# A clip handed from VectorE to GpSimd in the tile loop of a gated mixture of experts

## The reference, cut to what matters

```python
def swiglu(h):
    g = jnp.minimum(h[..., ::2], LIMIT)
    l = jnp.clip(h[..., 1::2], -LIMIT, LIMIT)        # the clip of the linear part, LIMIT = 7
    return g * jax.nn.sigmoid(ALPHA * g) * (l + 1.0)
...
h1 = jnp.einsum('td,efd->etf', xt, w1) + b1[:, None, :]
h3 = jnp.einsum('td,efd->etf', xt, w3) + b3[:, None, :]
a = swiglu(h1 * h3)
y = jnp.einsum('etf,edf->etd', a, w2) + b2[:, None, :]
routed = jnp.einsum('te,etd->td', cw, y)              # cw: two experts of eight for each token
```

## Time and profile before

| what | value |
|---|---|
| timed runs, median (lowest to highest) | 2465.71 us (2459.22 to 2470.34) |
| profiled execution, first to last instruction | 2596.9 us |
| mean granted TensorE clock in it | 0.812 of full speed |
| PE, DVE, ACT, POOL busy in it | 2013.5, 1771.5, 1399.1, 1150.4 us |
| second phase of the first gated mixture, first to last clip | 172.16 to 305.41 us |
| second phase of the second, first to last clip | 1186.53 to 1318.5 us |
| POOL busy from 171.25 to 315.74 us | 76.11 us in 78 transfers |
| POOL busy from 1185.62 to 1328.08 us | 76.42 us in 78 transfers |

### The profile page before, as it was taken

The page is one execution under the profiler, slowest core; times in us unless marked ns, Lnnn a source line. Parts: engine busy times, 40 slices in busy tenths (PEclk is TensorE's granted clock), DMA queues, the critical chain, the costliest instruction groups (busy, mean ns, idle before and its releaser), DMA issues. The chain is left out here.

```text
span 2596.9 us, 85429 instructions
## 1 busy us (share of the span) xinstructions
PE 2013.5 (78%) x34490; PEld 1682.7 (65%) x34490; DVE 1771.5 (68%) x4346; ACT 1399.1 (54%) x2304; POOL 1150.4 (44%) x1073
## 2 busy tenths in 40 slices
PE   3767569999999998577738899564666689768895
PEld 2557468888888887456726799452222278647895
DVE  4666578888888888666755444676999965454443
ACT  1546534444455554345725455257999956545452
POOL 3645545666656665463535466355000000045463
PEclk8778889999999999578868999786555556669997
DMA  5122310000000000012241222202333220021324
GB/s 123 39 77 72 92 58 1 0 0 0 0 0 0 0 0 2 22 58 76 73 149 49 73 76 63 76 1 35 63 53 61 49 65 8 3 91 42 86 78 122
DMA packets 112885, 125.53 MB, mean 48 GB/s; under 512 B 24248, under 2 KB 94504, under 8 KB 112064
## 3 DMA queue, kind: packets, MB, share of 16 engines
q1 hardware_dynamic: 91760, 84.85, 13.5%
q0 software_dynamic: 18176, 37.79, 4.4%
q10 hardware_dynamic: 2768, 0.55, 0.2%
HBM read 60.00 MB, written 46.20 MB: 41 GB/s over the span
## 5 line engine op out<-in xcount | busy, mean ns | idle before, releaser
L2623 DVE CUSTOM_DVE_ANT_0 be_logs<-be_joint,be_logs 128x1024 f32<-128x1024 f32 x256 | 293.3, 1220 | 10.2 <-ACT be_logs L2606 9.1
L2606 ACT ACTIVATE be_logs<-be_joint,b_tiny 128x1024 f32<-128x1024 f32 x256 | 283.8, 1114 | 19.6 <-PE be_joint L2591 11.8
L2591 PE MATMUL be_joint<-be_parts_k,be_parts_q 64*128 64x512 f32 x512 | 202.3, 789 | 108.8 <-DVE be_sums L2623 91.4
L451 POOL DMA_INDIRECT d_pairs<-s_y_tile,s_x_tiles x156 | 178.0, 1141 | 128.1 <-DVE s_y_tile L1426 101.8
L2591 PEld LDWEIGHTS be_joint<-be_parts_k,be_parts_q 64*128 64x128 f32 x512 | 73.7, 285 | 237.3 <-DVE be_sums L2623 216.5
L451 POOL DMA_INDIRECT d_pairs<-g_y_tile,g_x_tiles x156 | 152.5, 978 | 166.6 <-ACT g_y_tile L901 122.5
L1260 PE MATMUL s_ps_y<-s_down,s_a_tile 128*128 x1248 | 151.8, 275 | 0.0
L1426 DVE TENSOR_SCALAR s_y_tile<-s_ps_y,s_x_tiles 128x128 f32<-128x128 f32 x156 | 47.6, 347 | 147.8 <-PE s_ps_y L1260 100.8
L1260 PEld LDWEIGHTS s_ps_y<-s_down,s_a_tile 128*128 128x128 f32 x1248 | 145.9, 192 | 0.0
L1540 PE MATMUL m_front<-m_xnT,m_w_rot 128*128 128x128 f32 x1024 | 143.4, 284 | 3.2 <-DVE m_turned_q L1857 3.2
L1336 ACT ACTIVATE s_a_tile<-s_ps_h,s_tile_bias 128x256 f32<-128x256 f32 x312 | 122.3, 475 | 32.8 <-PE s_ps_h L1243 32.6
(11 more groups left out here) (504 smaller groups left out, 6271.2 us busy)
## 6 DMA issues: line engine op xcount, KB each, us to landing
g_x_tiles<-d_rows SPq DMA_DIRECT2D x78, 132.0 KB
s_x_tiles<-d_rows SPq DMA_DIRECT2D x78, 132.0 KB
bw_v<-b_v SPq DMA_DIRECT2D x64, 68.0 KB, 2.1
d_rows<-d_rows SPq DMA_DIRECT2D x32, 132.0 KB
s_down<-L_ffn_We SPq DMA_DIRECT2D x16, 256.0 KB, 5.4
be_parts_q<-be_high_q SPq DMA_DIRECT2D x64, 64.0 KB, 2.3
be_parts_q<-b_soft_q SPq DMA_DIRECT2D x64, 64.0 KB, 2.3
be_parts_k<-be_high_k SPq DMA_DIRECT2D x60, 64.0 KB, 2.3
```

The lines of the kernel that those rows point to most:

```text
L451: nc.gpsimd.indirect_dma_start(out=pairs[:, :], out_offset=bass.IndirectOffsetOnAxis(ap=x_tile[i % LOADS_AHEAD][:, h, D:D + 1].bitcast(U32 ...
L2591: last = nc.tensor.matmul(joint_ps[k % DEPTH][:, a, :], parts[b % 2][0][rows, i * P:(i + 1) * P], parts[b % 2][1][rows, half * 512:(half + ...
L2606: nc.scalar.activation(logs[k % DEPTH][:, :, :], joint_ps[k % DEPTH][:, :, :], ACT.Ln, bias=A.tiny[:, :]).then_inc(s.log_ready, 1)
L2623: nc.vector.tensor_tensor_reduce(out=flat, in0=joint_ps[k % DEPTH][:, :, :].rearrange("p a j -> p (a j)"), in1=flat, scale=1.0, scalar=0.0 ...
```

## The change

The clip at line 1055 leaves DVE's queue and comes into POOL's, as a new function `tile_linear` with the same two operations on the same 128x256 elements. POOL's order in the second phase becomes: clip of tiles 0, 1, 2; from then on, for i from 3 to 38, the two transfers of tile i-3 and the clip of tile i; at the end the transfers of tiles 36, 37, 38. The clip waits for the linear product of its tile, and for `a_tile` of two tiles earlier, which read the same buffer. On DVE the second half of the product gains a wait for the clip of two tiles earlier, which reads the buffer that this half writes.

```diff
-            for i in range(MAX_TILES):
+            def tile_linear(i):
+                b = i % 2
+                pool.wait_ge(s.tile_prod_l, i + 1)
+                wait(pool, s.tile_a, i - 1)
+                nc.gpsimd.tensor_scalar(linear_tile[b][:, :], prod_tile[b][:, 1, :], 7.0, -7.0, ALU.min, ALU.max).then_inc(s.tile_linear, 1)
+
+            for i in range(MAX_TILES):
+                if i > 2:
+                    dispatch.pool_tile_back(pool, i - 3, K.pairs, x_tile, y_tile)
+                tile_linear(i)
+            for i in range(MAX_TILES - 3, MAX_TILES):
                 dispatch.pool_tile_back(pool, i, K.pairs, x_tile, y_tile)
...
                 for part in range(2):
                     dve.wait_ge(s.tile_third, 2 * i + part + 1)
-                    if part == 0:
-                        wait(dve, s.tile_sig, i - 1)
+                    wait(dve, s.tile_linear if part else s.tile_sig, i - 1)
...
-                dve.wait_ge(s.tile_prod_l, i + 1)
-                nc.vector.tensor_scalar(linear_tile[b][:, :], prod_tile[b][:, 1, :], 7.0, -7.0, ALU.min, ALU.max).then_inc(s.tile_linear, 1)
```

## The result

The changed kernel takes 2500.22 us (median of 4 runs, 2494.51 to 2506.61) against 2468.03 for the kernel before (median of 4 runs): ratio 1.0131, 95% interval [1.0099, 1.0162], so 24 to 40 us slower. The forecast was 2533, in a range from 2455 to 2590. Slower was right, and so was the mechanism, POOL's pace; of the 67 us that the forecast added, 32 came.

What follows compares the result with a forecast made beforehand. The prediction took POOL's transfers, 2.52 us a tile, to pace the timed runs, and added 72 clips at 0.04 + 0.89 = 0.93 us, 67 us, to 2465.71 for 2533 us, in a range from 2455 to 2590.

Steps and rivals of the forecast that it cites:

- The holes: Gated tile phases: DVE's waits, such as 3.50 us, about every 10 us when recorded; timed runs taken to have none.
- a ceiling on the rate of work while it is recorded: Reason given for the gated phase's holes, which lift its mean from 2.5 to 3.5 us a tile.
- the span forecast: Recorded span of the changed kernel: to stay about 2590 to 2620 us while the median rises to 2533.
- DVE's relief is worth nothing: DVE's turn falls from 2.45 to about 2.24 us without gain, since POOL's 2.52 us stand above both.
- 36 clips a call count: Clips 3 to 38 stand between POOL's transfer pairs, 72 in all at 0.93 us: 67 us; clips 0 to 2 free.
- the price of the clip: POOL's 128x256 clip: 0.89 us, read half way between TENSOR_SCALAR rows of 0.559 us (128x128) and 1.564 us (128x512).
- The pauses: Around POOL's clip: 0.04 us ahead of it, 0.30 us behind it, with 0.76 us kept for the range.
- That DVE and POOL hold each other up: Tile phase: a clip waiting once for a DVE instruction of 0.42 us, up to 30 us more, inside the range.
- the cheap clip: Rival: POOL's clip costs 0.26 us like the cast, adding 22 us, 2487 us; chance 0.12.
- Holes of the kernel's own: Rival: timed runs have the gated phase's holes too, leaving POOL room for the clips; 7.6 us gained, 2458 us; chance 0.25.
- the dear clip: Rival: POOL's clip costs 1.564 us with a 0.76 us pause behind it, adding 148 us, 2614 us; chance 0.13.

Runs made afterwards that it cites:

- e2: Changed kernel with the linear part's clip left out on both engines, the product used unclipped: 2469.53 us, ratio 1.0010 to the kernel before.
- e1: The kernel before, unchanged, timed and recorded again for a second profile: 2467.36 us, ratio 1.0009.
- e5: Changed kernel with POOL multiplying by 0.5 in place of clipping, same size and place: 2544.98 us, ratio 1.0302 to the kernel before.
- e4: The changed kernel, unchanged, timed again beside the kernel before: 2506.38 us, ratio 1.0154 to the kernel before.

## Why the prediction came out as it did

- *The holes*: that the timed runs have none was right, and POOL's phase is 98.7 us without them (98.3 said); with e2, POOL and not DVE set the pace. The reason given, a ceiling on the rate of work while it is recorded, was wrong: e1 was recorded and has none. So this step came right partly by luck, and the span forecast from it, 2590 to 2620 us, missed (2504.8). What made the holes in the first recording stays open.
- *DVE's relief is worth nothing*: right (e2). DVE waits 1.04 us a turn for the clip; about 1 us was said, but by luck, from a pace of 3.45 us and a DVE turn of 2.24, where 3.12 and about 2.08 came.
- *36 clips a call count*: right. Those ahead of the first transfer cost at most about 1 us, the first pair starting at 160.75, after a wait for ACT, against 159.72 in e1.
- *The failed step is the price of the clip*: "I take 0.89, because the two neighbours are the same operation." They were the same opcode and other operations: a multiplication and a comparison of integers. The clip is a minimum and a maximum and takes 0.395 us. For a multiplication of that size 0.89 is near (0.867 in e5), though one of the two rows is none. This is a term of the sum mis-sized, 72 x (0.89 - 0.395) = 36 us too much; with 0.395 the prediction's own sum is 2465.71 + 72 x (0.04 + 0.395) = 2497.
- *The pauses*: 0.07 ahead of the clip for 0.04, 0.27 behind it for 0.30. Right to 0.01 in sum.
- *That DVE and POOL hold each other up* was kept for the range, at most 30 us, and left out of the sum. The form named there, a clip that waits for a DVE instruction, doesn't show: all clips last 394 to 405 ns. What is there is a longer transfer, 0.12 us a turn under the multiplication, 9 us; another 0.035 us, 2.5 us, for the transfer behind a computation had no term. The Trainium skill (SBUF — State Buffer, section Who interferes with whom) was cited for it; the trace agrees for the CAST (1.17 us when it began 0.05 us earlier) and for work with one operand from PSUM, which that section lets pass (0.96, or 0.995 behind a computation). For `tensor_tensor` with both inputs in SBUF it infers, though, that it doesn't hold up the making of a DMA's descriptors; here another operation with two such inputs, the multiplication (`scalar_tensor_tensor`), goes with 442 transfers of 1.10 or 1.22 us on the mean, so that inference doesn't carry over to it, and the measurement decides.
- *The sum again*, from measured terms: 72 x (0.07 + 0.395 + 0.27 - 0.30 + 0.155) = 42.5 us, to 2466.4 + 42.5 = 2509; measured 2506 and 2500.
- *The rivals*: the cheap clip (0.26 us, 2487) was nearer in price than the forecast, and stood on the cast's row and on the Trainium skill (GPSIMD Engine Reference, section Engine selection): one-input work "roughly line-rate". For minimum and maximum, 0.83 ns an element beside the cast's 1.01, the runs agree; for the multiplication, (1.564 - 0.867) / 256 = 2.7 ns (2.4 if the 0.07 us of the column in the longer row is taken off), they don't. That a row of the same name spoke against the rule was taken for more than it was; the smaller of the two, 0.559 / 128 = 4.4 ns an element where "near 3 to 4" was read, is a comparison. Holes of the kernel's own, and the dear clip, are out by e1 and e4.

## What to carry to other kernels

Before you price an operation by a row, read in the code which arithmetic that row does: a profile's opcode does not tell a minimum from a multiplication, and on one engine these differed by a factor of two. Where an engine sets the pace with a chain of short transfers, an instruction put between them costs its own time and more: 0.38 us for one of a single column, which itself takes 0.18. The short pauses between the transfers are no room for it; the clip came on top of them. So move work to an engine that idles in that stage, and not by its share of the span. Record a profile again before you explain stalls that no program line accounts for.

## What the runs showed of the hardware

- GpSimd's TENSOR_SCALAR, f32, 128 partitions: minimum and maximum take 0.184 us for 1 column, 0.395 for 256, 0.608 for 512; with one bound from a column in SBUF 0.469 for 256; a multiplication 0.867 for 256 and 1.564 for 512.
- An indirect transfer of this phase lasts 0.96 us on GpSimd, 0.995 right behind a computation on GpSimd, and up to 1.28 when DVE at its start works on operands that are all in SBUF. In the changed kernel the two meet in nearly every turn, since both follow GpSimd's clip: DVE's multiplication begins 0.10 us after the clip ends, the transfer 0.27.
- Two recordings of one program spanned 2596.9 and 2454.1 us. In the longer, PE stood still 21 times for 1.25 to 4.57 us in POOL's transfer phases of the two gated mixtures, in the shorter not once for over 1.2 us; these phases hold 74 of the 143 us, the rest lies in other stages.
